# A two-layer graph kernel: GpSimd's gathers without pacing by TensorE, block ends without GpSimd's drain

## What is computed

```python
# layer 0
msgs = z[dst] @ Wd + z[src] @ Ws + edge_weight[:, None] * ww + bm
agg  = segment_max(msgs, dst)                      # 0 for a node without edges
x    = layernorm(x + relu(z @ W1a + agg @ W1b + b1) @ W2 + b2)
# layer 1
h, he  = x @ node_fc_W + b, edge_features @ edge_fc_W + b
a      = sum(h[src] * h[dst], -1)
g      = sigmoid(relu(he @ rel_att_W1 + b1) . rel_att_W2 + b2)     # three relations
alpha, beta = seg_softmax(a, dst), seg_softmax(g, dst)
h_att  = segment_sum(alpha * (h[src] @ node_att_W[k]), dst) / 3    # summed over k
h_rel  = segment_sum(beta_m * (h[src] @ rel_att_W[m]), dst) / 3    # summed over m
out    = layernorm(x + gate * h_out + (1 - gate) * x)              # h_out = relu([h_att, h_rel] @ outW + b)
```

## Time and profile before

| | |
|---|---|
| time, median of 3 runs | 2283.71 us (2282.62 to 2285.59) |
| the profiled execution, from its first to its last instruction | 2723.8 us |
| mean clock granted to PE in it | 0.806 of full speed |
| busy in it: PE, DVE, ACT, POOL | 1843.7, 1328.7, 1115.3, 1639.6 us |
| pass 1, first to last gather of the loop | 65.1 to 1198.3 us |
| pass 2, first to last gather | 1332.3 to 2605.2 us |

### The profile page before, as it was taken

One profiled execution on the slowest core, in us unless ns is written; L12 is line 12 of the kernel. 1 busy time (PEld: TensorE's weight loads), 2 busy tenths in 40 slices (PEclk: granted clock), 3 DMA queues, 4 the chain that ended last, 5 costly groups with the idle time before them and its releaser, 6 DMA issues. The chain is left out here.

```text
span 2723.8 us, 43235 instructions
## 1 busy us (share of the span) xinstructions
PE 1843.7 (68%) x9891; PEld 1146.6 (42%) x9891; DVE 1328.7 (49%) x5220; ACT 1115.3 (41%) x3305; POOL 1639.6 (60%) x1705
## 2 busy tenths in 40 slices
PE   4577777677767777655666766676776776766665
PEld 3122222222222222114355655565665665655565
DVE  3454555554444444324535544544544545445459
ACT  1233333333333333333544444444444444444448
POOL 3666666666767777646455655555565655555525
PEclk7689888888889888876867777777777777777788
DMA  8433333333333333323311221221112221211113
GB/s 228 144 120 124 109 116 118 125 109 109 121 109 114 101 123 110 124 80 87 116 46 47 54 51 48 52 51 49 51 51 50 53 52 49 52 48 50 49 44 119
DMA packets 115983, 235.04 MB, mean 86 GB/s; under 512 B 32909, under 2 KB 68230, under 8 KB 106422
## 3 DMA queue, kind: packets, MB, share of 16 engines
q0 software_dynamic: 52832, 109.39, 16.3%
q1 hardware_dynamic: 56522, 97.21, 9.7%
q10 hardware_dynamic: 6540, 27.42, 2.9%
HBM read 166.01 MB, written 67.89 MB: 86 GB/s over the span
## 5 line engine op out<-in xcount | busy, mean ns | idle before, releaser
L463 POOL DMA_INDIRECT d_region<-d_h,d_region x784 | 747.8, 954 | 534.2 <-issue 221.1
L209 POOL DMA_INDIRECT acc<-d_src_product,b_region x784 | 779.4, 994 | 378.6 <-issue 225.5
L651 PE MATMUL banks<-acc,b_region 64*128 64x512 f32 x1176 | 351.8, 706 | 213.9 <-ACT acc L756 99.4
L859 DVE SCALAR_TENSOR_TENSOR acc<-b_region,acc 128x128 f32<-128x128 f32 x784 | 271.4, 346 | 433.6 <-DMA acc<-d_src_product,b_region 416.8
L1577 DVE TENSOR_TENSOR acc<-acc,banks 128x160 f32 x784 | 252.5, 322 | 318.6 <-remote 124.0
L1376 PE MATMUL banks<-d_region 128*128 128x128 f32 x1568 | 306.0, 357 | 4.1 <-issue 3.8
L1379 PE MATMUL banks<-d_region,pick 128*128 128x128 f32 x1568 | 294.1, 346 | 11.6 <-issue 11.2
L651 PEld LDWEIGHTS banks<-acc,b_region 64*128 64x128 f32 x1176 | 109.8, 211 | 429.7 <-issue 188.3
L1379 PEld LDWEIGHTS banks<-d_region,pick 128*128 128x128 f32 x1568 | 277.4, 262 | 13.6 <-issue 13.4
L1376 PEld LDWEIGHTS banks<-d_region 128*128 128x128 f32 x1568 | 271.2, 260 | 10.3 <-issue 5.3
L870 DVE SCALAR_TENSOR_TENSOR acc<-acc,b_region 128x128 f32<-128x128 f32 x784 | 270.1, 345 | 7.5 <-remote 5.2
(11 more groups left out here) (261 smaller groups left out, 2450.3 us busy)
## 6 DMA issues: line engine op xcount, KB each, us to landing
d_runs<-acc SPq DMA_DIRECT2D x48, 1024.0 KB
acc<-ea ACTq DMA_DIRECT2D x25, 1024.0 KB
acc<-d_src_product,b_region POOLq DMA_INDIRECT x784
d_region<-d_h,d_region POOLq DMA_INDIRECT x784
d_region<-d_rel SPq DMA_DIRECT2D x49, 256.0 KB
hT<-xT SPq DMA_DIRECT2D x7, 448.0 KB, 6.9
d_src_product<-acc SPq DMA_DIRECT2D x7, 448.0 KB, 3.7
acc<-xrow SPq DMA_DIRECT2D x1, 3136.0 KB
```

The lines of the kernel that those rows point to most:

```text
L209: pool.indirect_dma_start(self.rows[:, s, j, :], None, d["B"], bass.IndirectOffsetOnAxis(self.idx[:, k:k + 1], 0)).then_inc(self.gathered[ ...
L463: pool.indirect_dma_start(rows[:, s, :], None, table, bass.IndirectOffsetOnAxis(idx[:, s:s + 1], 0)).then_inc(gathered[q], 16)
L651: last = nc.tensor.matmul(bank[4 + n % 2 * 2 + h][:, :], wf[h * DE:(h + 1) * DE, m * P:(m + 1) * P], ea[h * DE:(h + 1) * DE, u % (2 * UC), ...
L859: nc.vector.scalar_tensor_tensor(rows[:, s, j, :], wwb, wgt[:, k:k + 1], rows[:, s, j, :], ALU.mult, ALU.add).then_inc(ch, 1)
```

## The change

Three edits. All five blocks are opened with `no_gpsimd_drain=True`, so that GpSimd's DRAIN ahead of each barrier is gone; the barrier stays. In pass 1 the waits on dt and tm go, and the wait on ch stays. In pass 2 the waits on hcp, tp and pt go, with the split of a group into halves; those on idxr and ug stay. No transfer, no product and no other engine's list is changed, and the number and the order of GpSimd's gathers stay.

In GpSimd's list at the end of pass 1, before the change: `L209 DMA` is a gather, `L103 ISA` clears semaphores, L596 and L599 are the mending, the branch of L519 is the block's end, the branch of L1013 the start of the next phase. b_dots_done is dt, b_mlp_product is tm, b_chain is ch.

The diff, cut (the block's line is changed alike in all five phases):

```diff
-        block = ctx.enter_context(nc.Block())
+        block = ctx.enter_context(nc.Block(no_gpsimd_drain=True))
...
@@ gather_rows @@
     for q in range(NG):
-        if q in PRODUCTS_BY:
-            pool.wait_ge(products_done, PRODUCTS_BY[q])
-        if q in TURNED_BY:
-            pool.wait_ge(rows_turned, TURNED_BY[q] + NG)
         gathers(q)
...
     with pool.Fori(0, rest) as it:
         for q in range(NG):
-            pool.wait_ge(rows_turned, it * NG + (NG + q - LAG + 1 + NG))
             pool.wait_ge(idx_ready, it * NG + (NG + q + 1))
             pool.wait_ge(rows_used, it * NG + (NG + q + 1))
-            gathers(q, range(0, GJ // 2))
-            pool.wait_ge(weights_turned, it * NG + (NG + q - LAGW + 1 + NG))
-            gathers(q, range(GJ // 2, GJ))
+            gathers(q)
...
@@ phase_runs @@
                 if g >= RG:
                     pool.wait_ge(ch, r_done(4 * (g - RG) + 3))
-                u = g // 2
                 for j in range(GJ):
-                    if u > LEASH and (g % 2, j) == (0, 0):
-                        pool.wait_ge(dt, u - 3 if u >= LOOKS_FROM else u - LEASH)
-                    if u >= LOOKS_FROM and (g % 2, j) == (0, 2):
-                        pool.wait_ge(tm, M * u - 5)
-                    if u >= LOOKS_FROM and (g % 2, j) == (1, 1):
-                        pool.wait_ge(tm, M * u - 3)
-                    if u >= LOOKS_FROM and (g % 2, j) == (1, 3):
-                        pool.wait_ge(dt, u - 2)
                     runs.gather(pool, d, g, j)
```

More of the change, by code:

```diff
@@ L451, in iterations_but_one, with gather_rows @@
     return eng.value_load(t["nit"][0:1, 1:2], min_val=MINIT - 1, max_val=MAXIT - 1)
-def gather_rows(nc, pool, t, table, idx, rows, idx_ready, rows_used, rows_turned, weights_turned, gathered, after_first,
-                products_done, scored, spread):
+def gather_rows(nc, pool, t, table, idx, rows, idx_ready, rows_used, gathered, after_first):
     rest = iterations_but_one(pool, t)
@@ L489 @@
 RG = 6
[L490 to L493, removed]
 ST16 = 16
@@ L497 @@
 HB = 3
-LEASH = 4
-LOOKS_FROM = 12
 NE = 8
@@ L1282, in credit @@
                     nc.gpsimd.memset(start[:, n:n + 1], 0.0).then_inc(s, per * CREDIT)
-            gather_rows(nc, pool, t, d["h"], idx, rows, idxr, ug, tp, pt, gat, credit, hcp, sT, vv)
+            gather_rows(nc, pool, t, d["h"], idx, rows, idxr, ug, gat, credit)
             new_sems.clear_ended()
```

## The result

The changed kernel takes 2270.78 us (median of 4 runs, 2268.18 to 2276.62) against 2284.65 us of the kernel before (4 runs with it): a ratio of 0.9938, 95% interval 0.9920 to 0.9955. That is 14.2 us less, between 10.3 and 18.3. The prediction was 2268.6 us in a range of 2245 to 2289, faster with a chance of 0.67. The saved times in this text are worked from the ratio; the medians differ by a little more or less. The time came out as forecast; where it came from only in part, as the experiments show.

What follows compares the result with a forecast made beforehand. The prediction took GpSimd's own gathers to bound both passes. Drains -10.6, pass 1's waits -2.2 and pass 2's -2.3 us summed to -15.1, from 2283.7 to 2268.6 us, with a range of 2245 to 2289.

Steps and rivals of the forecast that it cites:

- The bound: Both passes: in the runs GpSimd's own gathers bind, since 2283.71 us is only 24.2 above a GpSimd that never waits.
- The waits: Pacing waits taken out of GpSimd's gathers: 2.2 us gained in pass 1 and 2.3 us in pass 2.
- the room: Both passes: what the pacing's waits can take of the runs' time, between 0 and 24.2 us.
- the long gathers: Both passes: by their means, gathers are 53.3 us longer in sum than at 0.94 us each, more than 24.2.
- one missed look: One unsatisfied pacing wait saved in each pass: 2.2 us in pass 1, 2.3 us in pass 2.
- the floor of 2259.5: Whole kernel: the span in us without any unsatisfied wait in the passes, summed from the profile's timeline.
- The rival that the waits are real: Both passes: the pacing's waits fill the whole 24.2 us in the runs, giving 2249 us; chance 0.17.
- The first drain: GpSimd's drain at the first block's end (L215): 2.2 us on the path, ending at 64.2 against DVE's 62.0.
- The bound of 9.8 us: First block's end: the upper bound of the gain there, where the whole gap at 65.08 would go.
- The second drain: GpSimd's drain at the second block's end (L519): all 8.4 us on the path, with 0 booked for time coming back.
- The last three drains: GpSimd's drains at the ends of the last three blocks: hidden behind other engines' work or the span's end, 0 each.
- Slower by collisions: Mainly pass 2: unpaced gathers collide more with DVE and reach pass 1's mean, 31.4 us more, around 2300; chance 0.17.

Runs made afterwards that it cites:

- second profile: A profile of an execution whose program is that of the kernel before, from a file whose new lines had no effect: span 2285.9 us; its runs 2287.41 us, ratio 1.0002.
- waits_only: The changed kernel with the five GpSimd drains put back, so only both passes' waits are edited: 2285.73 us against 2287.88 of before, ratio 0.9992.
- pass1_free: The kernel before with only pass 1's pacing waits taken out: 2289.27 us against 2289.59 of before, ratio 0.9995.
- pass2_only: The kernel before with only pass 2's pacing waits taken out: 2285.61 us against 2287.88 of before, ratio 0.9985.
- drains_late: The changed kernel with GpSimd's drains put back at the ends of the last three blocks: 2271.68 us against 2289.59 of before, ratio 0.9938.

## Why the prediction was right, and where not

**The bound: right.** The step that set the profile's 2723.8 us against the runs' 2283.71 and booked no gap of the profile as such is what kept the forecast near. The second profile shows it directly: POOL's idle time ahead of gathers is 247.4 + 248.5 us, the 0.30 us a gather, the first end's gap and some 10 us ahead of pass 2. GpSimd's own gathers are the bound in both passes, before and after.

**The waits: the size was wrong, 4.5 us against nothing.** The prediction had the room as 0 to 24.2 us and the long gathers as the rival claim on it, and then took one missed look in each pass, from the mean of waits in a profile it had just called unreliable. The second profile has 50 us of long gathers (39 ns above 940 in pass 1 and 25 in pass 2, times 784). The room itself was taken too small, since the floor of 2259.5 had in it the long execution's stretches outside the passes, 19 us longer than in the second profile; the long gathers fill 24.2 + 19 = 43 us as well, so nothing was left for waits. waits_only, pass1_free and pass2_only measure 1.8, 1.1 (both indistinguishable from 0) and 3.4 us (at the edge). A slip in the same part, which changes nothing: groups 2 to 7 are 24 gathers, 30.0 us, not 28 and 34.9. The rival that the waits are real, 2249 us, has fallen with them.

**The first drain: the size was wrong, 2.2 us against 7.7 by the gap (6.2 and 8.3 by the runs).** The step that failed is the sentence that the blocks' ends are no loop and so carry little of the 440 us. The first end carried much: DVE's last work there was some 8 us late in that execution (62.0 against 54.2), which hid most of a drain that is otherwise open. The bound of 9.8 us for this gap, which the prediction kept as its other end, was the better value.

**The second drain: 8.4 us, right, in a kernel that has both.** Its row is the same in each of five traces, and the gap behind the barrier came out at 2.32 us where 2.4 was forecast. That its cost does not come back at the first gather behind the barrier was right as well. Two things were not foreseen: that its length depends on the first drain, which does not hurt the sum, since both go; and that taking the first drain away costs 1.3 us ahead of the mending's store, where the prediction booked nothing.

**The last three drains: 0, right,** by drains_late, as near as the runs tell.

**So the sum of 15.1 us was near 14.2 by luck, through two errors that cancel:** the drains are worth 14.8 us by the rows (14.9 by the runs) instead of 10.6, the waits nothing that shows instead of 4.5.

**Slower by collisions: fell.** The mean gather is 981 and 962 ns after, 979 and 965 in the second profile of before; the 40 ns by which the passes differed in the first profile are 14 there. Long gathers exist on both sides. One of the changed kernel and the one ahead of it, with what DVE does beside the long one:

```profile
63.80 0.94 POOL L209 DMA_INDIRECT acc<-d_src_product,b_region  x1 [0.30 <-issue]
65.05 3.90 POOL L209 DMA_INDIRECT acc<-d_src_product,b_region  x1 [0.30 <-issue]
```

```profile
64.90 0.34 DVE L836 SCALAR_TENSOR_TENSOR acc<-b_region,acc 128x128 f32<-128x128 f32 x1
...
67.79 0.33 DVE L847 SCALAR_TENSOR_TENSOR acc<-acc,b_region 128x128 f32<-128x128 f32 x1
```

DVE's instructions with two inputs stand back to back from before the gather's start to 67.79 + 0.33 = 68.12, and the gather ends 0.83 us behind the last of them, close to the 0.94 us that a gather takes by itself. By itself this gather agrees with the rule of the Trainium skill, page "SBUF — State Buffer", section "SBUF: two separate sides", that one of the two engines blocks until the other is done. But DVE's row of such instructions runs from 62.00 on, and the gathers at 62.55 and 63.80 took 0.94 us each beside it; so the trace agrees only in part, as with the earlier trace rows. In the second profile of before, with the pacing, one gather of 4.49 us lies in the same place of the pass. The means show no effect of the pacing, and the 2300 us of this rival did not come. What makes a gather long stays open: no run here takes the collisions away.

**The signs named ahead.** No DRAIN of POOLq at the five ends: seen. No wait on PE in pass 1: seen, but in the second profile there is hardly one before either. The gap at the first end "about 7.5": wrong, 0.75. Means within 10 ns of 994 and 954: missed for pass 1 (981), because 994 was the long execution's.

## What to carry to other kernels

When a profiled execution is far longer than the runs, none of its waits is evidence by itself, those at the ends of blocks included: here the 8.4 us at the second end held, and the 2.2 at the first did not. Take a second profile of the same program before costing a wait by it. A drain of GpSimd's queue ahead of a barrier cost here what it took beyond the last of the other engines and GpSimd's own last gather: look at each block's end by itself, since of five two were open (some 8 us each) and three cost nothing that shows. A wait that is satisfied when it is reached left the gap at 0.30 us, so pacing that does not bind can go or stay.

## What was not expected of the hardware

The drain's length is no constant: 0.56 us in the last block, which has no indirect transfers; for the second drain 7.74, 8.39 and 8.72 us with 766, 774 and 778 transfers since the first, or 28, 20 and 16 ahead of it, 82 ns a transfer; 1.87 us with 794 transfers and no drain before. And the first drain ended 2.7 us behind the end of the last gather with 16 and with 28 transfers ahead of it (one run each), but 7.1 to 8.9 us with 20. Leaving out the first drain therefore changes the price of the second, and adds 1.3 us ahead of the mending's store; the price of a single one can't be read from a kernel that has both.
